# A gated cross-attention and expert layer: first norm and key stores in another order, four waits of products moved, key weights over two queues

## The chip, the cores and the metric

The kernel runs on one core of a Trainium2 chip. The metric is the device time of one execution in microseconds (us), the median of several runs. PE is the matrix engine, DVE the vector engine, ACT the scalar engine, POOL GpSimd, and SP the sync engine, which only issues transfers. PEld is PE's loading of stationary operands. ACTq, SPq and POOLq are the same engines' queues of DMA issues.

## What is computed

x has 8 sequences of 512 rows of 512 numbers, the context 8 sequences of 120 rows of 512. Cut to what matters:

```python
xn = layernorm(x)
Q = heads(xn @ Wq.T + bq); K = heads(ctx @ Wk.T + bk); V = heads(ctx @ Wv.T + bv)   # 16 heads of 32
a  = softmax(Q @ K.T / sqrt(32)) @ V
e  = mean over 8 experts of (a @ We[i].T + be[i])
x  = x + tanh(g_xattn) * (e @ Wo.T + bo)
hs = layernorm(x).reshape(4096, 512)
probs = softmax(hs @ w_gate); best = argmax(probs)       # 8 experts
keep the first 100 rows of each expert, in order of rows; gate = probs[best]
out = x + tanh(g_ffn) * (gate * (hs @ w_expert + b_expert) for the kept rows, else 0)
```

## The kernel before

Every product in full precision is made of three products of float16 parts (high by high, high by low, low by high), each 128 by 128 against up to 512 columns. The mean over the experts and Wo are folded into one 512 by 512 matrix ("mix"). Each engine runs its own list of steps in the order written in the kernel, and steps of different engines meet at semaphores (`wait_ge`).

**Prologue.** The list `units` (lines 369 to 656) holds 52 first and 6 late units. A unit is some transposes or products by PE into one of eight PSUM banks, and then a cast of the high part by ACT and the low part by DVE. A bank is taken again by the unit eight places later, once its casts are over. In order: the four tiles of Wk turned, the bias rows, the context tiles turned, K of sequences 0 to 3 (lines 459 to 479), Wv, K of sequences 4 to 7, Wq, V of sequence 0, Wo (`woT`, four units), `wogT` (line 522, Wo by the gate's weights), V of sequences 1, 2 and 3, the first sequence's normalised rows x tiles 0 and 1 turned (`x_unit`), `wog` (line 545, which reads `wogT`'s two parts), V of 4 (`v4`), `cb` (which reads `wog`), `bias_part`, x tiles 2 and 3, V of 5, `mix_bias`, V of 6. The late units are V of 7, the mix matrix in four parts, and `gateT`. They are woven into the first steps of sequence 0.

SP issues the loads (lines 734 to 766): the four Wk tiles of 256 KB, the context, and then the other weights, x and the eight experts' weights. POOL sums the experts' weights (`sum_we`), and after the first of these sums makes the first sequence's `rstd` and `x0_shift`. ACT issues the loads of three bias vectors (lines 1235 and 1236), goes through its casts of the units (lines 1274 to 1282), and has three other pieces of work between them:

- `store_k(half)` (lines 1238 to 1246): 12 DMA issues that write K's parts to DRAM, from where SP loads them as a stack. `first_units_over` (line 664) waits for all 24 of them. PE calls it ahead of the second Q product of sequence 0, and SP, POOL and DVE call it too, at the end of the prologue.
- `first_rows()` (lines 1259 to 1268): two small scalings of `tanh_g`, and the four activations that normalise the first sequence's rows into `xn`, once `x0_shift` is there.
- `be_part_high()`, a cast.

```python
if units[i]["done"] == made["wogT"]:
    store_k(1)
    first_rows()
prepare(0, i)
```

**A sequence.** For each sequence b the attention is done in four groups g of four heads. `scores` (line 879) makes the scores of a group in four banks, in two halves. The first half waits for ACT's first half of exponentials of the group before (`s_ex2`), the second for their second half (`s_ex`). `exp` on ACT turns them into `probs`. `weight_sums` (line 899) sums the weights into `den_b`, and `value_sums` (line 915) makes the weighted values in `num_b`. In the first call, (0, 0), `weight_sums` waits with `prologue_over` (line 670) for all late units. The products of sequence b+1's Q and the routing (`route_x`, line 948; `gate_mix`, line 930, in sequence 0, which waits for ACT's `part_x`) are woven between. Sequence by sequence DVE chooses each row's expert, `places` (line 1083) counts the rows per expert on PE after DVE's `choose` (`base_cnt`), DVE reads the counts (`read_places`: `place_all`), makes `place_hot`, and PE adds to a table of rows (`table_rows`, for sequence 6 split in `table_token` and `table_values`, lines 1109 to 1118).

**The tail.** In sequence 7's list (line 1215) PE also does the expert's product for the kept rows of the first seven sequences (`row_product`, 0 to 7, 12 products each, rows gathered by POOL), and then `last_product` for the last sequence's rows in five parts. Each needs a result of DVE (`row_out`) that frees its bank. DVE's and ACT's own lists for that stretch stand at lines 1866 and 1417. POOL scatters the rows and SP stores the last sequence.

PE's steps in sequence 7 begin with

```python
(scores, 0, 1), (weight_sums, 0, 0), (table_token, -1, 0), (value_sums, 0, 0), (scores, 0, 2),
```

and the end of the row products is

```python
(row_product, 0, 6), (places, 0, 0), (row_product, 0, 7), (last_product, 0, 0), ...
```

Of the kernel before, what the change touches and what calls it, by code (L numbers as in the profile page):

```python
# [49 lines left out]
P = 128  # L50
# [35 lines left out]
def build(nc, x, ctx, g_xattn, g_ffn, Wq, bq, Wk, bk, Wv, bv, We, be, Wo, bo, w_gate, w_expert, b_expert, out):  # L86
# [8 lines left out]
    with ExitStack() as st:  # L95
# [631 lines left out]
        def _(e):  # L727
# [6 lines left out]
            def load_tiles(n, w):  # L734
                for i in range(NK):
                    load(slots[slot_of[n]][:, i, :], w[i * P:(i + 1) * P, :], s_wt[n][i])

            load_tiles("wkT", Wk)
# [99 lines left out]
        def _(e):  # L838
# [60 lines left out]
            def weight_sums(b, g):  # L899
                e.wait_ge(s_ex, 4 * b + g + 1)  # L900
                if g == 0:
                    if b == 0:
                        prologue_over(e)
                    e.wait_ge(s_lraw, b)
                    e.wait_ge(s_sh, b + 1)
                for h in range(2):
                    sel = den_sel[:, (h * NK + g) * DK:(h * NK + g + 1) * DK]
                    for j in range(HJ):
                        row = slice(j * DK, (j + 1) * DK)
                        ins = mm(den_b[row, 0:SH], sel, probs[:, g % 2, j, h * SH:(h + 1) * SH],  # L910
                                 start=(g == 0 and h == 0), stop=(g == NK - 1 and h == 1))
                if g == NK - 1:
                    ins.then_inc(s_den, 1)

            def value_sums(b, g):
                if (b, g) == (B - 1, 3):
                    e.wait_ge(s_ex, 4 * B)
                elif g:
                    e.wait_ge(s_num, 4 * b + g)
# [28 lines left out]
            def route_x(b, _):  # L948
# [6 lines left out]
                if b == 0:  # L955
                    e.wait_ge(s_route, 3)
                elif b == 1:
                    e.wait_ge(s_qhi, 4)
                    e.wait_ge(s_qlo, 4)
# [245 lines left out]
            def last_product(_, i):  # L1205
# [10 lines left out]
                (scores, 0, 1), (weight_sums, 0, 0), (table_token, -1, 0), (value_sums, 0, 0), (scores, 0, 2),  # L1216
# [7 lines left out]
                (places, 0, 0), (row_product, 0, 7),  # L1224
# [6 lines left out]
        def _(e):  # L1231
            def act(out_, in_, func=ACT.Copy, **kw):
                return e.activation(out_, in_, func, **kw)  # L1233

            for i, b_ in enumerate((bq, bk, bo)):
                e.dma_start(bias_rows[i * NK:(i + 1) * NK, :], b_.rearrange("(t p) -> t p", p=P)).then_inc(s_bqk, 16)
# [37 lines left out]
            for i in range(N_FIRST):  # L1274
                if units[i]["done"] == made[("wvT", 2)]:
                    be_part_high()
                if units[i]["done"] == made["wogT"]:
                    store_k(1)
                    first_rows()
                prepare(0, i)  # L1280
# [781 lines left out]
```

## Time and profile before

| | |
|---|---|
| median of 3 runs | 415.07 us (415.05 to 415.48) |
| the profiled execution: its own time | 413.09 us |
| its span | 411.4 us |
| PE busy | 400.2 us, 97% of the span |
| DVE busy | 336.1 us, 82% |
| ACT busy | 228.3 us, 55% |
| POOL busy | 166.8 us, 41% |
| chain that ended last | PE 84%, DVE 6%, ACT 3%, issue 3%, DMA 1% |

Times in the rows below are from the start of the span. A timeline row gives the start in us, the length in us, the engine, the line, the operation, what it writes from what, the shape and the count, and, in square brackets, how long the engine was idle before it and what was done last of what it waited for. A row of several instructions gives the length from the first one's start to the last one's end. Idle time that ends in "issue" was ended by nothing that the profile shows. Matrix products overlap: the next one starts before the one before has ended. The granted clock is PE's share of full speed.

### The profile page before, as it was taken

To read this page: it belongs to the slowest core of one execution; us is meant where nothing else is said; L and a number is where in the kernel's file an instruction comes from. 1 tells how busy PE (TensorE), PEld (TensorE's weight loads), DVE (VectorE), ACT (ScalarE), POOL (GpSimd) and SP (SyncE) were. 2 spreads that over 40 slices of the span, in tenths; PEclk is the share of its full clock that TensorE was granted. 3 is DMA by queue.
4 is the path that set the end of the run, shared out by engine and by line. 5 is a ranking of instruction groups with operands and counts; after the bars stand their busy time and mean duration, and the time that the engine had idled before them with its cause. 6 is when DMAs were issued, how large, how long until landed. Compare 5 with 4: busy or idle time off the path is not lost.

```text
span 411.4 us, 8771 instructions
## 1 busy us (share of the span) xinstructions
PE 400.2 (97%) x3126; PEld 190.5 (46%) x3126; DVE 336.1 (82%) x683; ACT 228.3 (55%) x320; POOL 166.8 (41%) x154
## 2 busy tenths in 40 slices
PE   8999989999999999999999999999999999999987
PEld 4556554444444444444444444444444445354434
DVE  7449267886897989988998999899896688779994
ACT  5434422668465854947585485748457474774200
POOL 2028999115090347309033530803361072550460
DMA  8999981366048507824870692386059026232584
GB/s 278 325 387 398 385 320 37 81 124 169 2 102 175 199 1 160 220 95 88 148 237 3 144 228 104 71 170 235 1 131 239 4 55 174 73 114 47 107 169 148
DMA packets 65517, 63.19 MB, mean 154 GB/s; under 512 B 41765, under 2 KB 45233, under 8 KB 65475
## 3 DMA queue, kind: packets, MB, share of 16 engines
q1 hardware_dynamic: 60363, 56.19, 49.8%
q0 software_dynamic: 1632, 3.49, 3.1%
q10 hardware_dynamic: 3480, 2.96, 2.2%
q8 instruction: 26, 0.43, 0.5%
q14 instruction: 16, 0.13, 0.1%
HBM read 29.59 MB, written 12.98 MB: 103 GB/s over the span
## 4 chain that ended last, share of the span: by engine, by line
PE 84%; DVE 6%; ACT 3%; issue 3%; ACTq 1%; DMA 1%; SPq 0%; DVEq 0%
PE ps L840 71%; PE ps L456 7%; PE ps L588 3%; PE ps L405 2%; ACTq L1244 1%; DMA raw<-in_L_xattn_Wk_dram 1%; DVE xb L1565 1%; DVE rows L1820 1%; ACT xn L1233 1%; DVE bn_raw L1571 1%; ACT xb L1233 1%; DVE xn_lo L1808 1%; ACT woT_hi L397 0%; ACT mixT_hi L397 0%; DVE q_stack L1838 0%
## 5 line engine op out<-in xcount | busy, mean ns | idle before, releaser
L1233 ACT ACTIVATE probs<-ps 120x1024 f32<-120x1024 f32 x64 | 62.0, 1023 | 21.0 <-PE ps L840 20.9
L1599 DVE TENSOR_REDUCE neg_max<-ps 128x16 bf16<-128x1920 f32 x32 | 68.6, 2143 | 3.7 <-PE ps L840 3.7
L1985 POOL TENSOR_TENSOR attn_lo<-attn,attn_hi 128x512 f16<-128x512 f32 x28 | 31.8, 1158 | 92.0 <-ACT attn_hi L1233 92.0
L840 PE MATMUL ps<-xnT_hi,wqT_hi 128*128 128x512 f16 x128 | 48.6, 380 | 0.0
L840 PE MATMUL ps<-mixT_hi,attn_hi 128*128 128x512 f16 x128 | 48.6, 380 | 0.0
L840 PE MATMUL ps<-mixT_lo,attn_hi 128*128 128x512 f16 x128 | 48.5, 379 | 0.0
L840 PE MATMUL ps<-xnT_lo,wqT_hi 128*128 128x512 f16 x128 | 48.5, 379 | 0.0
L1993 POOL TENSOR_TENSOR xb<-xb,mix_bias 128x512 f32<-128x512 f32 x32 | 39.6, 1272 | 17.5 <-DVE cb_col L1542 17.5
L1233 ACT ACTIVATE q_hi<-ps,bias_cols 128x512 f16<-128x512 f32 x32 | 22.0, 688 | 31.5 <-PE ps L840 31.5
L840 PE MATMUL ps<-q_stack,k_stack 97*120 97x512 f16 x128 | 34.9, 390 | 0.1
L840 PE MATMUL ps<-probs,den_sel 120*32 120x256 f32 x512 | 34.1, 384 | 0.8 <-issue 0.8
L840 PE MATMUL ps<-probs,v_all 120*32 120x512 f32 x256 | 33.5, 595 | 0.0
L840 PE MATMUL ps<-mixT_hi,attn_lo 128*128 128x512 f16 x128 | 33.0, 380 | 0.0
L840 PE MATMUL ps<-xnT_hi,wqT_lo 128*128 128x512 f16 x128 | 32.8, 379 | 0.0
L1233 ACT ACTIVATE attn<-ps 128x512 f32<-128x512 f32 x32 | 19.0, 594 | 21.3 <-PE ps L840 21.3
L1233 ACT ACTIVATE q_stack<-q_hi 32x2048 f16<-32x2048 f16 x16 | 30.5, 1907 | 0.5
L1593 DVE SCALAR_TENSOR_TENSOR q_lo<-ps,bias_cols,q_hi 128x512 f16<-128x512 f32 x32 | 23.9, 746 | 5.2 <-ACT q_hi L1233 5.0
L1559 DVE TENSOR_TENSOR attn<-ps,attn 128x512 f32<-128x512 f32 x32 | 20.6, 685 | 7.8 <-PE ps L840 7.5
L1233 ACT ACTIVATE attn_hi<-attn 128x512 f16<-128x512 f32 x32 | 19.7, 627 | 12.6 <-DVE attn L1559 12.6
L1565 DVE SCALAR_TENSOR_TENSOR xb<-ps,xb 128x512 f32<-128x512 f32 x32 | 21.9, 683 | 2.8 <-PE ps L840 2.4
L840 PEld LDWEIGHTS ps<-q_stack,k_stack 97*120 97x120 f16 x128 | 14.4, 132 | 20.3 <-issue 11.1
L1924 POOL TENSOR_SCALAR veps<-mv 128x4 f32<-128x4 f32 x8 | 1.8, 228 | 51.0 <-DVE mv L1474 50.9
(277 smaller groups left out, 805.6 us busy)
## 6 DMA issues: line engine op xcount, KB each, us to landing
xb<-in_x_dram SPq DMA_DIRECT2D x8, 1024.0 KB, 6.6
q_stack<-q_hi SPq DMA_DIRECT2D x48, 128.0 KB, 2.4
out_dram<-xb SPq DMA_DIRECT2D x6, 1024.0 KB, 6.5
raw<-in_L_xattn_We_dram SPq DMA_DIRECT2D x5, 1024.0 KB, 11.2
q_stack<-q_lo SPq DMA_DIRECT2D x32, 128.0 KB, 2.4
xb<-in_L_xattn_We_dram SPq DMA_DIRECT2D x3, 1024.0 KB, 9.8
k_stack<-k_scratch SPq DMA_DIRECT2D x8, 360.0 KB, 4.3
k_scratch<-k_hi ACTq DMA_DIRECT2D x16, 120.0 KB, 6.7
```

What stands on the lines that cost most here:

```text
L405: ins = e.transpose(b[0:rows, i * cols:(i + 1) * cols], src_of(i), ident[0:cols, 0:cols])
L456: ins = e.matmul(out_, a(pa, k), b(pb_, k), start=(i == 0), stop=(i == len(steps) - 1))
L588: ins = e.matmul(b[:, :], left(i, o), right[j][:, o, :], start=(n == 0), stop=(n == len(steps) - 1))
L840: return e.matmul(out_, a, b, start=start, stop=stop, **kw)
L1233: return e.activation(out_, in_, func, **kw)
L1244: e.dma_start(k_scratch[bs, part * DK:(part + 1) * DK, j, :].rearrange("b d s -> d b s"), src[j * DK:(j + 1) * DK, bs, :, :].rearrange("d ...
L1559: e.tensor_tensor(attn[:, g, :], (den_b, num_b)[g % 2], attn[:, g, :], ALU.mult).then_inc(s_at, 1)
L1565: e.scalar_tensor_tensor(out=row, in0=pair_b[t % 2], scalar=1.0 / (ATTN_SCALE * MIX_SCALE), in1=row, op0=ALU.mult, op1=ALU.add).then_inc(s ...
L1593: e.scalar_tensor_tensor(out=q_lo[:, g, :], in0=pair_b[g % 2], scalar=bias_cols[:, g:g + 1], in1=q_hi[:, g, :], op0=ALU.add, op1=ALU.subtr ...
L1599: e.tensor_reduce(neg_max[:, :, :, g], quad[:, :, 0:NT * SK].rearrange("p j (t s) -> p t j s", t=NT), AX.X, ALU.max, negate=True).then_inc ...
L1985: e.tensor_tensor(attn_lo[:, g, :], attn[:, g, :], attn_hi[:, g, :], ALU.subtract).then_inc(s_alo, 1)
L1993: ins = e.tensor_tensor(row, row, mix_bias[:, :], ALU.add)
```

## The change

It has these parts:

- A. Wk's tiles 1 and 3 are issued by ACT, ahead of its three bias loads. SP issues tiles 0 and 2.
- B. On ACT `first_rows()` is moved to before the cast of `woT`'s first tile, and `store_k(1)` to after `wogT`'s cast.
- C. `weight_sums(0, 0)` on PE waits for the last of the four mix units and no longer for all late units. The wait for all of them is made ahead of `route_x(1)`, the first use of the bank of `gateT`.
- D. In sequence 7 `value_sums(7, 0)` is done before `table_token`, with a wait for DVE's reading of the counts of sequence 6, which are in the same bank.
- E. `places(7)` comes after `row_product` 7 and no longer before it.

```diff
-            def load_tiles(n, w):
-                for i in range(NK):
+            def load_tiles(n, w, tiles=range(NK)):
+                for i in tiles:
                     load(slots[slot_of[n]][:, i, :], w[i * P:(i + 1) * P, :], s_wt[n][i])
 
-            load_tiles("wkT", Wk)
+            load_tiles("wkT", Wk, (0, 2))
...
                 if g == 0:
                     if b == 0:
-                        prologue_over(e)
+                        for s_, n in made[("mix", NK - 1)]:
+                            e.wait_ge(s_, n)
...
             def value_sums(b, g):
                 if (b, g) == (B - 1, 3):
                     e.wait_ge(s_ex, 4 * B)
+                elif (b, g) == (B - 1, 0):
+                    e.wait_ge(s_plr, B - 1)
                 elif g:
                     e.wait_ge(s_num, 4 * b + g)
...
                 if b == 0:
                     e.wait_ge(s_route, 3)
                 elif b == 1:
+                    prologue_over(e)
                     e.wait_ge(s_qhi, 4)
                     e.wait_ge(s_qlo, 4)
...
             run([B - 1], [
-                (scores, 0, 1), (weight_sums, 0, 0), (table_token, -1, 0), (value_sums, 0, 0), (scores, 0, 2),
+                (scores, 0, 1), (weight_sums, 0, 0), (value_sums, 0, 0), (table_token, -1, 0), (scores, 0, 2),
...
-                (places, 0, 0), (row_product, 0, 7),
+                (row_product, 0, 7), (places, 0, 0),
...
+            for i in (1, 3):
+                e.dma_start(slots[slot_of["wkT"]][:, i, :], Wk[i * P:(i + 1) * P, :]).then_inc(s_wt["wkT"][i], 16)
             for i, b_ in enumerate((bq, bk, bo)):
...
+                if units[i]["done"] == made[("woT", 0)]:
+                    first_rows()
+                prepare(0, i)
                 if units[i]["done"] == made["wogT"]:
                     store_k(1)
-                    first_rows()
-                prepare(0, i)
```

## Rows read from the trace of the kernel before

**Rows 1.** Stretches: PE, PEld, DVE, ACT, POOL busy us; clock; DMA share; GB/s.

```profile
1.90:5.00 3.10, 3.10 (x15) 1.53 (x13) 2.65 (x15) 1.87 (x3) 1.52 (x10) 1.00 0.94 274
95.00:351.00 256.00, 255.88 (x2210) 115.03 (x2202) 224.11 (x451) 161.72 (x215) 93.72 (x90) 1.00 0.49 124
```

**Rows 2.** List of waits, PE alone: us in total, times, longest us.

```profile
PE ps L840 <- DVE base_cnt L1650: 1.7, 1, 1.7
...
PE ps L840 <- DVE place_hot L1721: 1.0, 1, 1.0
```

**Rows 3.** Timeline, 39 to 54 us: start us, us, engine, line, operation.

```profile
39.16 0.24 POOL L1972 TENSOR_SCALAR x_shift<-x_shift 128x4 f32<-128x4 f32 x1
...
41.50 0.31 ACTq L1244 DMA_DIRECT2D k_scratch<-k_hi  x1
...
46.19 1.79 ACTq L1244 DMA_DIRECT2D k_scratch<-k_lo  x4
...
48.36 2.93 ACT L1233 ACTIVATE xn<-xb,x_shift,rstd 128x512 f32<-128x512 f32 x4
...
51.87 0.69 DVE L398 SCALAR_TENSOR_TENSOR sum_lo<-ps,sum_hi 128x512 f16<-128x512 f32 x1 [8.41 <-ACT sum_hi L397]
...
52.81 0.17 PE L534 MATMUL ps<-gate_sum,sum_hi 128*128 128x8 f16 x1 [1.63 <-ACT xnT_hi L397]
...
53.58 0.40 PE L456 MATMUL ps<-mixT_hi,ctxT_hi 128*120 128x512 f16 x1 [0.42 <-DVE v_all L492]
```

**Rows 4.** Tile k_lo's DMAs up to 60 us; timeline of POOL and PE.

```profile
DMA to landing us min/median/max: 7.0/9.5/12.4
...
63.00 4.51 POOL L1960 TENSOR_TENSOR w_sum<-w_sum,xb 128x2048 f32<-128x2048 f32 x1
...
66.83 0.38 PE L840 MATMUL ps<-xnT_hi,wqT_hi 128*128 128x512 f16 x1
```

**Rows 5.** Timeline, DVE, PE and ACT, 92 to 102 us.

```profile
92.29 0.75 DVE L599 SCALAR_TENSOR_TENSOR mixT_lo<-ps,mix_scale,mixT_hi 128x512 f16<-128x512 f32 x1 [1.32 <-ACT mixT_hi L598]
93.32 0.75 DVE L610 SCALAR_TENSOR_TENSOR part_lo<-ps,gate_scale,part_hi 128x512 f16<-128x512 f32 x1 [0.28 <-ACT part_hi L609]
...
94.28 1.07 PE L840 MATMUL ps<-probs,den_sel 120*32 120x256 f32 x16 [0.81 <-issue]
...
100.32 0.59 ACT L1233 ACTIVATE part_x<-ps 128x512 f32<-128x512 f32 x1
...
101.64 0.17 PE L840 MATMUL ps<-gate_sum,part_hi 128*128 128x8 f16 x1
```

**Rows 6.** Timeline, ACT and PE's weight loads, 354 to 357 us.

```profile
354.75 1.92 ACT L1233 ACTIVATE probs<-ps 120x1024 f32<-120x1024 f32 x2
...
356.72 0.18 PEld L840 LDWEIGHTS ps<-q_stack,k_stack 97*120 97x120 f16 x2 [0.39 <-ACT probs L1233]
```

**Rows 7.** Timeline, PE and DVE, 390 to 398 us; DVE's waits from 372 us.

```profile
392.31 1.03 PE L840 MATMUL ps<-wqT_hi,q_stack 128*128 128x512 f16 x4
...
395.14 0.38 PE L840 MATMUL ps<-wqT_hi,q_stack 128*128 128x512 f16 x1
...
397.72 0.38 PE L840 MATMUL ps<-wqT_hi,q_hi 128*128 128x512 f16 x1
...
390.49 0.74 DVE L1826 SCALAR_TENSOR_TENSOR rows<-ps,coef,rows 100x512 f32<-100x512 f32 x1
...
394.89 0.75 DVE L1826 SCALAR_TENSOR_TENSOR rows<-ps,coef,rows 100x512 f32<-100x512 f32 x1
...
DVE xb L1863 <- PE ps L840: 2.7, 4, 1.2
```

**Rows 8.** Timeline, SP's issues and PE, the first 12 us.

```profile
0.79 1.89 SPq L729 DMA_DIRECT2D raw<-in_L_xattn_Wk_dram  x4
...
5.87 0.63 PE L405 MATMUL ps<-ident,raw 128*128 128x128 f32 x4 [0.80 <-DMA raw<-in_L_xattn_Wk_dram]
...
11.33 0.37 PE L456 MATMUL ps<-ctxT_hi,wkT_hi 128*128 128x480 f16 x1
```

## The prediction

> **What bounds the kernel now.** I read the busy times by stretch first: from 95 to 351 us PE works 255.88 of 256 us, and the next engine, DVE, 224.11 [rows 1]. So the end is set by PE's work and by the gaps in it, and moves only if a gap closes. Then the list of what PE waited for [rows 2]: eight entries, the longest 1.7 us. They lie in the prologue, at the turn to sequence 7 and in the tail, and each part of the change lies at one of them. The third view, the timelines around each gap, says what ended it and what comes next. They are needed because a gap that closes is worth only the time until the next late thing. The granted clock of 1.00, 2.4 GHz [rows 1], leaves nothing to the clock.
>
> **The change, part by part.** The sums are made against the profiled execution (span 411.4 us, its own time 413.09 us); the median of the runs shown is 415.07, 1.98 us above it, and I carry savings over unchanged.
>
> *Part B, first rows' norm ahead of the key stores.* PE's 1.6 us gap before the `wog` unit is a wait for `wogT`'s casts, not for the xn casts that the list names: `wogT` ends on DVE at 51.87+0.69 = 52.56 us, and PE starts at 52.81, after 1.63 us idle [rows 3]. Those casts sat on ACT behind 12 store issues (from 41.50 to 47.98 us) and four norm activations (2.93 us) [rows 3]. After the change ACT first does the norm. Its two tiny scalings fit while ACT still waits for `woT`'s transposes; the last input, `x0_shift`, is ready at 39.16+0.24 = 39.40 us [rows 3]. So the norm runs 39.4 to 42.35, the four `woT` casts (some 0.5 us each) to 44.4, `wogT`'s cast to 45.0, and DVE's low parts end by about 46.1. PE asks at 52.81-1.63, about 51.2, five us later. `woT`'s casts, 2.2 us later than before, free banks that PE takes again only for the x tiles, near 50; the cover is `wogT`'s product and three value products. The gap closes: 1.63 us. Behind it PE shows 0.42 us more before `v4`, at 53.58 [rows 3]. By the code `v4` has fifteen waits, all satisfied by then; the other value products have as many and none shows such a gap, so I read it as the sequencer's time, seen only because PE stood. It goes with the stall. I take 2.05, low bound 1.63.
> What is late next: the 12 store issues (6.5 us) now start at 45.0 and end near 51.4, and x tiles 0 and 1 are cast only then, until 52.5. DVE ends `wog`'s column near 53.4; PE needs it after `v4`, at 51.3+2.6 = 53.9. Slack half a microsecond. The stores end 3.4 us later; those of `k_lo` took 9.5 us to land in the median and 12.4 at most [rows 4], so 63.8 at worst, and PE comes to the wait on all stores at 66.83-2.05 = 64.8 [rows 4]. SP's loads of K, POOL's memset of `k_stack` and DVE stand behind the same wait, with one microsecond of slack or more. POOL's expert sum ends at 63.00+4.51 = 67.5 [rows 4] and doesn't move; ACT reads it only after the casts of the first two Q products and the routing, the second of which PE begins at 64.8 now, so about 69; 1.5 us in time.
>
> *Part C, the prologue's wait.* The sums of weights of sequence 0 wait for all late units, the last of which DVE ends at 93.32+0.75 = 94.07; PE starts at 94.28 after 0.81 us of idleness. Now they wait for the last mix unit alone, which DVE ends at 92.29+0.75 = 93.04, before PE's scores end at 94.28-0.81 = 93.47 [rows 5]. The 0.81 closes, but other engines don't move here: ACT's cast of the routing part stands at 100.32+0.59 = 100.91 behind norm work that doesn't depend on PE, and `gate_mix`, at 101.64 before, would now ask at 100.8 [rows 5]. That takes back about 0.16. I take 0.65; ends 0 (ACT's and DVE's pace takes all) and 0.85. The full wait, now ahead of the next routing product, two score steps later, was met at 94.07 and costs nothing.
>
> *Part D, sequence 7's first value products ahead of the token table.* PE stood 1.0 us for DVE's `place_hot` [rows 2]; now the products fill that. But the scores of g=3 need the exponentials of g=2: ACT starts those at 354.75, right behind a small exponential that waits for DVE's `l_sub`, and ends at 354.75+1.92 = 356.67. PE's second half of those scores starts at 356.72 [rows 6]: it waits for ACT already. None of these inputs is moved by D, so PE arrives a microsecond earlier and stands there. Worth 0; ends 0 and 1.0. The added wait is for `place_all`, which DVE makes before `place_hot`; behind it stand only the value products and the table, which has to wait for `place_hot` in any case.
>
> *Part E, row product 7 ahead of `places`.* PE stood 1.7 us for DVE's counts. Row product 6's last matmuls start at 392.31, four at 0.216 us, so row product 7 can start at 393.17 and not at 395.14; its input rows and its bank's reader are done (DVE's fourth row, 390.49+0.74) [rows 7]. It takes 397.72-395.14 = 2.58 us, `places` 0.1, and the last products start at 395.85 and not at 397.72: 1.87 us. They need row 4 from DVE, 394.89+0.75 = 395.64 [rows 7], just in time. DVE reads `places` only after three more row outputs, as before. Is DVE the bound then? In the tail it waited 2.7 us in all for PE [rows 7], more than 1.87, so PE still leads, by 0.8 us. I take 1.85, low bound 0.9 (row outputs late), high bound 1.95.
>
> *Part A, Wk tiles on two queues.* PE waited for tile 2, whose transposes start at 5.87 [rows 8]. Tile 2's issue comes one place earlier (issues are 0.47 us apart: 1.89 us for four [rows 8]), tile 3's two places earlier; 0.45 us is the gain if issue limits. But from 1.9 to 5.0 us the DMA engines are 94% busy at 274 GB/s [rows 1]: bytes limit as much as issues. The Trainium skill, "DMA: Bandwidth & Descriptors", section "Issuing engines are not separate DMA queues", says that DMAs issued on several engines interleave on the same 16 DMA engines and save only issue time. By that rule tile 0 would land with tile 1 and tile 2 with tile 3. Interleaved, tile 2 lands when tile 3 does now; PE's transposes of tile 3 take their turn 0.63 us after those of tile 2 began [rows 8], so the loss is at most about 0.6 us. From 5.87 to 11.33 PE runs without a real gap, so either shift passes on whole. Between -0.45 and +0.6 I take 0, since both ends are about as near. The bias rows, now two issues later on ACT, are used only behind tile 3's transposes; ACT's table load, two issues later too, has the wait of ACT's first cast for PE as its cover.
>
> **Sum:** 2.05+0.65+0+1.85+0 = 4.55 us; 413.09-4.55 = 408.5 for the profiled execution, 415.07-4.55 = **410.5 us** for the median. After 95 us PE has no gap to take the savings up until 351, and DVE, ACT and SP follow PE's steps there.
>
> **Rivals.**
> 1. *The tiles interleave*. For: the DMA shares. Against: SP's issues are still spared. PE's transposes of tiles 2 and 3 come 0.6 later: 410.5+0.6 = 411.1. Chance 0.22. It is the rule of the Trainium skill's page on DMA that stands behind this case.
> 2. *C is swallowed*: ACT's and DVE's work on the norm of sequence 2 isn't moved and PE meets it. For: DVE's norm waits for POOL there. Against: PE meets that chain in one place only by my reading. 410.5+0.65 = 411.2. Chance 0.12.
> 3. *B only moves the wait*: the stores' issue takes longer or x casts come later than PE's 53.9, and the `wog` column becomes what is late. Against: half a microsecond of slack. All of 2.05 lost: 410.5+2.05 = 412.6. Chance 0.11.
> 4. *D is worth its microsecond*, if ACT's small exponential comes earlier than I think: 410.5-1.0 = 409.5. Chance 0.08.
> 5. *Slower*: the stores. ACT issues them 3.4 us later into DMA engines that still carry the expert weights, and PE, SP, POOL and DVE all wait for the last one before sequence 0. The price is nothing until it lands after 64.8, and each microsecond later costs one; it turns the balance at 64.8+4.55 = 69.4 us, 18 us after its issue, where the slowest now takes 12.4. For 416.5 it would take 20 us. Chance 0.03.
> 6. *The change doesn't do what it says*, no gap closes: 415.1. Chance 0.02.
>
> **How the numbers follow.** The forecast, A even and the other gaps closed as summed, has the rest, 0.42. The range 409.3 to 412.2 holds it with rivals 1, 2 and 4, 0.84 together, and leaves out rival 3. A difference under 0.2% (0.8 us) can't be told from none. Faster by more: forecast and rivals 1 to 4, 0.95; within 0.2%: 0.02; slower: 0.03.
>
> **What would show it.** Right: no PE wait before `wog` and before `v4`, twelve stores issued from 45 us on; the sums of weights of sequence 0 right behind the scores, a wait of 0.1 to 0.2 at `gate_mix`; about 0.7 us of idle PE before the g=3 scores of sequence 7 in place of 1.0 before the table; no PE wait near 388 (393 before), last products without a gap. Wrong: a PE wait for `wog`'s DVE column, any new PE wait between 60 and 350 us, a wait for rows in the last products, or PE's first K product more than 0.3 us later than its 11.33 now.

## The result and the profile after

The changed kernel takes **408.98 us** in the median (407.06 to 409.04, 5 runs); the kernel before, with the two runs that were added to the three shown ahead, 415.05 us (412.36 to 415.48, 5 runs). The ratio is 0.9852, 95% interval 0.9813 to 0.9891: 6.1 us less, 1.5%. The prediction was 410.5 with a range of 409.3 to 412.2: the direction was right, the size too small, and the result lies below the range.

The profiled execution of the changed kernel took 407.45 us with a span of 405.9 (before 413.09 and 411.4), 5.64 us less. First its page and PE's list of waits (us in total, times, longest):

```profile
span 405.9 us, 8772 instructions
...
PE 398.9 (98%) x3126; PEld 190.4 (47%) x3126; DVE 336.0 (83%) x683; ACT 227.7 (56%) x320; POOL 166.9 (41%) x154
```

```profile
PE ps L855 <- POOL ones_bf L1903: 1.1, 1, 1.1
PE ps L405 <- DMA bias_rows<-in_L_xattn_bo_dram: 1.0, 1, 1.0
PE ps L840 <- ACT probs L1237: 0.8, 2, 0.5
PE ps L405 <- DMA raw<-in_L_xattn_Wk_dram: 0.5, 1, 0.5
PE ps L840 <- issue: 0.2, 1, 0.2
PE ps L456 <- DVE mixT_lo L398: 0.2, 1, 0.2
```

The waits for `base_cnt` (1.7 us) and `place_hot` (1.0) [rows 2] are gone, and so is the one ahead of `wog`. New are a wait of 1.0 us for the bias rows and two for ACT's exponentials. The timeline at the old `wog` gap, to be held against [rows 3]:

```profile
39.70 2.94 ACT L1237 ACTIVATE xn<-xb,x_shift,rstd 128x512 f32<-128x512 f32 x4 [1.81 <-POOL x_shift L1979]
42.27 0.31 ACTq L1250 DMA_DIRECT2D k_scratch<-k_hi  x1
...
45.61 0.68 DVE L398 SCALAR_TENSOR_TENSOR sum_lo<-ps,sum_hi 128x512 f16<-128x512 f32 x1
46.76 2.61 ACTq L1250 DMA_DIRECT2D k_scratch<-k_lo  x4
...
49.88 1.04 PE L405 MATMUL ps<-ident,xn 128*128 128x128 f32 x8
50.76 0.17 PE L534 MATMUL ps<-gate_sum,sum_hi 128*128 128x8 f16 x1
...
50.96 0.41 PE L456 MATMUL ps<-mixT_hi,ctxT_hi 128*120 128x512 f16 x1
```

`wogT` is ready at 46.29 and not at 52.56, PE asks at 50.76, and `v4` follows `wog` after 0.20 us. Then the other places, for [rows 5], [rows 6] and [rows 7], and DVE's waits in the tail:

```profile
90.79 0.64 PE L840 MATMUL ps<-probs,den_sel 120*32 120x256 f32 x8
...
98.35 0.18 PE L840 MATMUL ps<-gate_sum,part_hi 128*128 128x8 f16 x1
...
351.41 1.92 ACT L1237 ACTIVATE probs<-ps 120x1024 f32<-120x1024 f32 x2
...
352.47 0.64 PE L840 MATMUL ps<-q_stack,k_stack 97*120 97x512 f16 x2 [0.50 <-ACT probs L1237]
353.38 0.64 PE L840 MATMUL ps<-q_stack,k_stack 97*120 97x512 f16 x2 [0.27 <-ACT probs L1237]
...
391.55 1.03 PE L840 MATMUL ps<-wqT_hi,q_stack 128*128 128x512 f16 x4
392.41 0.18 PE L840 MATMUL ps<-choice,tri 128*128 128x32 bf16 x1
...
392.46 0.38 PE L840 MATMUL ps<-wqT_hi,q_hi 128*128 128x512 f16 x1
...
DVE xb L1870 <- PE ps L840: 1.0, 2, 0.8
```

Idle times in the list overlap with the modelled end of the last product, so I set the two traces against each other by **starts of the same PE instruction**. These are the distances, in us, and what changed:

| stretch, PE start to PE start | before | after | change |
|---|---|---|---|
| start of the span to the first K product | 11.33 | 11.07 | -0.26 (A) |
| first K product to the x tiles | 38.82 | 38.81 | -0.01 |
| x tiles to `v4` | 3.43 | 1.08 | -2.35 (B) |
| `v4` to the first sums of weights | 40.70 | 39.83 | -0.87 (C) |
| sums of weights to `gate_mix` | 7.36 | 7.56 | +0.20 (C, given back) |
| `gate_mix` to sequence 7's logits | 241.70 | 241.65 | -0.05 |
| logits to the table's products | 13.86 | 13.86 | 0 (D) |
| table's products to the last products | 40.52 | 38.60 | -1.92 (E) |
| last products to DVE's last end | 11.07 | 11.07 | 0 |
| from there to the end of the span, and outside it | 4.30 | 3.92 | -0.38 (A, see the end of "Why the prediction was wrong") |

The sum, 5.64, is that of the profiled executions. The median fell by 0.43 more, which this table can't show; that is the second half of the study.

### The profile page after: what moved, and what is told of

It is laid out like the page before. It is cut to its first block, busy times and chain, and to the rows that moved or that the text cites. A ratio compares the mean times of both kernels' runs of the same rounds, so it can differ in the third digit from the quotient of the medians.

```text
span 405.9 us, 8772 instructions
## 1 busy us (share of the span) xinstructions
PE 398.9 (98%) x3126; PEld 190.4 (47%) x3126; DVE 336.0 (83%) x683; ACT 227.7 (56%) x320; POOL 166.9 (41%) x154
## 4 chain that ended last, share of the span: by engine, by line
PE 93%; DVE 2%; ACT 1%; DMA 1%; issue 1%; ACTq 1%; POOL 0%; DVEq 0%
PE ps L840 77%; PE ps L456 9%; PE ps L588 3%; PE ps L405 2%; DMA bias_rows<-in_L_xattn_bo_dram 1%; ACT probs L1237 1%; ACT mixT_hi L397 0%; PE ps L1164 0%; DVE xb L1572 0%; DVE mixT_lo L398 0%; POOL known L1933 0%; PE ps L606 0%; PE ps L525 0%; PE ps L855 0%; ACTq L1240 0%
```

## The experiments, part by part

Every kernel here is the kernel before or after with the lines shown. They ran in five sets, with the kernel before beside them in each; its median was 415.02, 415.81, 414.43, 414.77 and 414.83 us. A table of results stands at the end of the section after this one.

**A alone** (Wk's tiles 1 and 3 on ACT's queue, no other part).

> Part A alone on the kernel before. Theory 1 (read from the changed kernel's trace): tile 0 lands later, PE's first transposes start near 4.3 and not 3.6, the bias rows land near 7.8 and PE waits 1.0 us for them, and the first K product starts at 11.1 for 11.33: a gain of 0.3 us in the profile, of 0.2 to 0.5 in the median. Theory 2 (the two queues also calm the start of the load stream, which is why the medians moved 6.1 us and the profiles 5.5): a gain of 0.8 to 1.5 us in the median. Theory 3 (interleaving as forecast at worst): a loss of 0.5 us.

Measured: 413.46 us median (411.93 to 416.46, 10 runs), ratio 0.9975 (0.9946 to 1.0003), profiled 412.81. The start:

```profile
4.38 0.64 PE L405 MATMUL ps<-ident,raw 128*128 128x128 f32 x4 [0.59 <-DMA raw<-in_L_xattn_Wk_dram]
...
7.28 0.20 PE L405 MATMUL ps<-ident,bias_rows 12*128 12x12 f32 x1 [0.51 <-DMA bias_rows<-in_L_xattn_bo_dram]
...
10.49 0.36 PE L456 MATMUL ps<-ctxT_hi,wkT_hi 128*128 128x480 f16 x1
...
52.94 0.17 PE L534 MATMUL ps<-gate_sum,sum_hi 128*128 128x8 f16 x1 [2.17 <-ACT xnT_hi L397]
```

Tile 0 is 0.76 us later than before (3.62), no tile keeps PE waiting after that, and the K products start 0.84 us earlier. At `wog` nothing of it is left: 52.94, before 52.81. There ACT's stores and norm set the time, and PE only waits 0.5 us longer. "Either shift passes on whole" held only with B beside it. The median is 1.6 us lower all the same, though the profile is lower by 0.3; what moves it is told with the clock below (seven of these ten runs kept it, one in three of the kernel before do), and whether A has a part in that stayed open. The 0.84 us itself can't be put down to A from this trace; see the starts of the other traces below.

**B alone.**

> Part B alone. Theory 1: PE's gaps there are longer from start to start than the list of waits says (1.78 and 0.57 us, not 1.63 and 0.42); v4 starts 2.35 us earlier than in the kernel before, at 51.2, and the time falls by 2.3 us. Theory 2 (my forecast, the listed idle times): 2.05 us. Theory 3: B needs A's or others' help, and gives under 1.7 alone.

Measured: 410.93 (410.45 to 411.38, 6 runs), ratio 0.991 (0.9879 to 0.994), profiled 410.95. From the x tiles to `v4` 1.08 us, as in the full change: B is worth 2.35 in the profile, of it 1.78 at `wog` (2.66 to 0.88) and 0.57 at `v4` (0.77 to 0.20). But its median is 4.1 us under the kernel before, nearly twice that, and the runs lie within 0.9 us where the kernel before spreads over 4. That was the first sign that a trace of one execution of the kernel before doesn't show all that its gap costs.

**The gap ahead of v4.** The kernel before, `v4` without its waits, all of which units ahead have made already:

```diff
-                for s_, n in u["needs"]:
+                for s_, n in [] if u["done"] == made[("v", 4)] else u["needs"]:
                     e.wait_ge(s_, n)
```

> The kernel before, without the fifteen waits of unit v4 (all on counts that PE has waited for before, in the units ahead). In the kernel before v4 starts 0.77 us after wog, with B 0.20 after. Theory of the prediction (the 0.57 is the sequencer's time for these waits, seen only because PE stood): the distance from wog to v4 falls to about 0.2 to 0.3 and the time by 0.5, to about 412.6 in the profile. Rival (the time is the fetch of instructions or something else behind a stall): it stays at 0.7 to 0.8. It also is one more sample of the stores' issue in the kernel before: 6.5 to 7.5 us and the wog unit at 52.8 to 53, or, by theory 1 of e10_stores_behind, up to 4 us later in an execution whose time is over 414.

Measured: one run, 412.48 us.

```profile
52.38 0.17 PE L534 MATMUL ps<-gate_sum,sum_hi 128*128 128x8 f16 x1 [1.37 <-ACT xnT_hi L397]
...
52.59 0.41 PE L456 MATMUL ps<-mixT_hi,ctxT_hi 128*120 128x512 f16 x1
```

`v4` stands 0.21 behind `wog` and not 0.77. So the fifteen waits, all met, took PE's sequencer 0.56 us, which shows where PE has run dry and the sequencer isn't ahead of it.

**The two halves of B.** The stores behind `wogT`'s casts, the norm at its old place:

```diff
                 if units[i]["done"] == made["wogT"]:
-                    store_k(1)
                     first_rows()
                 prepare(0, i)
+                if units[i]["done"] == made["wogT"]:
+                    store_k(1)
```

> The kernel before, with the key stores of the second half issued behind wogT's casts and not ahead of them, and ahead of them still the norm of the first rows, at its old place. Open is why the medians of the kernels with B lie some 4 us under the kernel before, while the profiled executions differ by 2.2. Theory 1 (the issue of the stores is what varies): the 12 DMA issues on ACT take 6.5 to 7.5 us and longer in many executions, and the kernel before pays every excess at the wog unit. Here they are off that path, though the norm (2.9 us) stays on it: norm and casts end near 45.5, PE asks at 51.2, so the distance from the x tiles to v4 is 1.1 us as in B alone, the profiled time near 411, the median 411 and the runs within 1 us of one another. Theory 2 (the spread comes from the start or from elsewhere, and B's excess in the median is chance): the profile is the same, but the runs spread over 4 us like those of the kernel before, with a median near 413.

The norm ahead of `woT`, the stores at their old place:

```diff
+                if units[i]["done"] == made[("woT", 0)]:
+                    first_rows()
                 if units[i]["done"] == made["wogT"]:
                     store_k(1)
-                    first_rows()
                 prepare(0, i)
```

> The other half of B: the norm of the first rows ahead of woT's casts, the 12 stores still ahead of wogT's casts. Without the norm between, wogT's high part comes 2.9 us sooner than 51.2, at about 48.3, and its low part at 49.7; PE asks at 51.2. With stores of 6.5 to 7.5 us the gap closes in the profile as in B (x tiles to v4 1.1 us). Theory 1 (the issue of the stores varies by up to 4 us between executions): 1.5 us of slack are not enough for the slow ones, so the runs spread more than in e10_stores_behind and the median lies 0.5 to 2 us above it, 411.5 to 413. Theory 2 (the norm was the costly part and the issues are steady): the same as in e10_stores_behind, median near 411, spread under 1 us.

Measured: 410.59 (410.17 to 411.5, 6 runs; ratio 0.9883, 0.9856 to 0.991) and 410.72 (410.18 to 411.87, 6 runs; 0.988, 0.9853 to 0.9906). Either half alone closes the gap (x tiles to `v4` 1.08 and 1.33 us) and makes the runs narrow. Stores and norm together are too long for the cover, each one alone is not. The theory that the stores' issue swings by up to 4 us between executions wanted the second kernel slower and wider; it isn't, so that theory falls: their issue took 6.2 to 7.7 us in all nine traces with twelve stores and norm in the old order. In the second kernel `v4` stands 0.46 us behind `wog`, though the list shows no wait before `wog`; that some of the fifteen waits' time shows there too is likely, not tested.

**All parts but D.**

> The changed kernel without part D. Theory 1: D is worth nothing; PE waits 1.0 to 1.4 us for place_hot before the token table of sequence 7, and the scores of g=3 end where they do with D; the time is within 0.2 us of the changed kernel's. Theory 2: D hides the 0.37 us that PE loses just before sequence 7's first scores, so without it the time is 0.3 to 0.5 us longer. Theory 3: D is worth the whole wait, 1.0 us longer without it.

Measured: 408.72 (407.34 to 409.15, 4 runs), ratio 0.9857 (0.9812 to 0.9902).

**D alone.**

> Part D alone. The prediction gave it nothing: PE no longer waits for place_hot (1.0 us), but the g=3 scores of sequence 7 wait for ACT's exponentials of g=2, so from the logits to the table 13.9 us as before, profile 413.1 and a median as of the kernel before. Rival: 1.0 us faster, if ACT's exponentials start sooner when PE isn't held up. One more sample of the wog gap.

Measured: 415.21 (413.01 to 416.06, 10 runs), ratio 1.0008 (0.998 to 1.0036). Logits to table 13.97 us without D in the one and 13.96 with it in the other, 13.86 in the traces before and after: no gain from D shows.

**E alone.**

> Part E alone. From the token table's values to the last products 40.52 us before; with E 38.6: 1.92 us, and nothing else moves, since it is the last part of the program: profile 411.2, median 1.9 under that of the kernel before (413.2 for 415.1). Rival (DVE leads in the tail once the gap is gone): 0.9 to 1.5. One more sample of the wog gap.

Measured: 412.3 (410.82 to 414.02, 10 runs), ratio 0.9947 (0.9921 to 0.9974), 2.1 us less; in the trace 38.61 us from the table's products to the last ones, 1.91 less.

**C alone**, measured twice.

> Part C alone. From v4 to the first weight sums 40.70 us before; with C 39.8, and 0.2 comes back at gate_mix: 0.67 in all, so a profile near 412.4 and a median 0.7 under that of the kernel before in the same call (414.4 for 415.1). Rival (with the gap at wog still there the late units stand otherwise and the whole 0.87 or nothing stays). One more sample of the wog gap.

> Part C alone once more. Its first four runs took 414.06, 415.23, 818.91 and 1427.73 us, the last two at a granted clock of 1.00, which no theory here explains. If that was a disturbance of the chip, all runs now lie between 411.8 and 416, with a median 0.7 under the kernel before in this call. If it is C's doing without B (a wait met late by a DMA), some run again takes far longer. The time from v4 to the first weight sums is 39.8 us in an execution without a fall of the clock, against 40.70.

Measured: the first time 414.06, 415.23, 818.91 and 1427.73 us. The second time 414.14 (412.2 to 415.83, 10 runs), ratio 0.9981 (0.995 to 1.0012), 0.7 us under the kernel before beside it, as the term says, but inside the interval; it is the trace and not the median that shows C's gain. The two long runs did not come back in ten; what made them was not found, and nothing rests on them. `v4` to the sums of weights took 41.35 and 41.50 us in C's two traces, where 39.8 was expected. That is the next thing.

## The experiments on the spread

The profiles of C alone (spans 412.3 and 412.6) and of D alone (414.3) have what the one before lacks: the granted clock falls behind the `wog` gap. D alone, PE's timeline, and stretches of it (PE busy us, clock, DMA share, GB/s):

```profile
54.36 0.17 PE L534 MATMUL ps<-gate_sum,sum_hi 128*128 128x8 f16 x1 [2.17 <-ACT xnT_hi L397]
...
56.00 0.38 PE L456 MATMUL ps<-mixT_lo,ctxT_hi 128*120 128x512 f16 x1
...
56.54 0.63 PE L456 MATMUL ps<-mixT_hi,ctxT_hi 128*120 128x512 f16 x1
56.97 0.63 PE L456 MATMUL ps<-mixT_lo,ctxT_hi 128*120 128x512 f16 x1
```

```profile
54.00:58.00 4.00, 3.22 (x18) 0.79 1.06 406
58.00:62.00 4.00, 3.93 (x42) 0.78 0.76 287
62.00:66.00 4.00, 4.00 (x20) 1.00 0.01 4
```

The same in the trace before:

```profile
54.00:58.00 4.00, 3.89 (x42) 1.00 1.06 406
58.00:62.00 4.00, 4.00 (x24) 1.00 0.42 160
```

PE stood for 2.17 us, went on for 1.9 us at full clock, and then products of 512 columns came 0.43 us apart instead of 0.216: 1.2 GHz in place of 2.4. Microsecond by microsecond the clock is 0.66 from 56 to 57 us, 0.50 to 59, 0.64 to 60 and then 1.00. The value products and mix units behind it are 1.42 us longer here (42.12 us to the sums of weights, 40.70 before). The Trainium skill, "TensorE: Matmul & The Clock Gate", "Part 1: The HAM clock gate", says that the lower clock is the default and that activity releases it. These rows agree: the clock falls behind the one long gap in the middle of the kernel and comes back while PE is busy.

Each run has its mean granted clock, so the runs of the kernel before can be sorted, 107 of them from the five sets and from the kernel before again:

| mean clock | runs | median us | from, to |
|---|---|---|---|
| 0.999 to 1.000 | 35 | 413.39 | 412.42 to 414.43 |
| 0.995, 0.996 | 58 | 415.22 | 413.99 to 417.39 |
| 0.991, 0.992 | 13 | 416.84 | 416.30 to 418.03 |

(One run more took 465 us at a clock of 0.849 and is left out.) A mean clock lower by 0.004 in a time of 413 us is about one such fall: 0.004 x 413 = 1.7 us lost, and the medians are 1.8 apart. The profiled execution of the kernel before, 413.09, belongs to the third without a fall; the three runs shown, 415.05 to 415.48, all took longer than any of the 35 without one. Of the 55 runs of kernels in which the gap is closed, by B or a half of it, 54 have a clock of 0.999 or 1.000.

**The kernel before again**, for a second trace and more runs.

> The kernel before, unchanged, for a second profiled execution of it and a second distribution of its times. Open is why its runs lie at 412 to 418 with a median near 415, while its profiled execution took 413.09 and those of kernels with the same order at the wog unit 412.8 (A alone) and 412.5 (v4 without its waits). Theory 1 (typical executions pay a longer stretch of store issues ahead of the norm): a profile of 414 or more shows the x tiles to v4 longer than 3.4 us by what its time is over 413. Theory 3 (profiled executions are faster than the timed ones at this place): the profile is again near 413 and the median near 415. Rival (the start of the run, the loads of Wk and the context): a slow profile shows its excess ahead of the first K product at 11.3 us.

Measured: 415.39 (412.58 to 417.53, 12 runs), ratio 1.0009 (0.9978 to 1.004). The profiled one had 413.64, clock 1.000, and a `wog` gap of 2.86 where the first had 2.66; its first K product is 0.40 later, from a wait for a context tile. So it was again an execution without a fall, which shows nothing of the slower ones.

**The gap 0.3 us shorter**, the last store issue moved behind `wogT`'s casts (`store_k` takes a range of its twelve issues):

```diff
                 if units[i]["done"] == made["wogT"]:
-                    store_k(1)
+                    store_k(1, 0, 11)
                     first_rows()
                 prepare(0, i)
+                if units[i]["done"] == made["wogT"]:
+                    store_k(1, 11, 12)
```

> The kernel before, with only the last of the twelve store issues moved behind wogT's casts: the gap at wog is shorter by one issue, 0.45 to 0.7 us (1.0 to 1.6 left of 1.6 to 2.2). Theory (clock): the granted clock stays at 0.999 to 1.000 in nearly all runs and the median falls by 1.5 to 2.5 us, three times and more the time taken off the gap: 412.5 to 413.3. Rival (the spread comes from elsewhere): median 0.5 us lower, low-clock runs as often as in the kernel before.

Measured: 414.39 (412.79 to 416.77, 12 runs), ratio 0.9997 (0.9971 to 1.0023). Five runs without a fall, seven with: no fewer falls than the kernel before had (seven of 16 without in this set). In its trace x tiles to `wog` are 2.37 us and not 2.66; the eleven issues left took 6.2 us where twelve had taken 6.5. A miss: the expectation was 1.5 to 2.5 us, and cutting the gap a little bought nothing that shows.

**The gap longer**, one norm activation done twice:

```diff
                 e.wait_ge(s_x0s, 2)
+                act(xn[:, 0, :], xb[:, 0, 0, :], ACT.Identity, scale=rstd[:, 0, 0:1],
+                    bias=x0_shift[:, 0:1]).then_inc(s_tanh, 1)
+                e.wait_ge(s_tanh, 3)
```

> The kernel before, with the first norm activation done twice (with a wait between) ahead of wogT's casts: 0.8 to 1.0 us more on ACT's chain into the wog gap. Theory (clock): this gap is where the granted clock falls (idle of 2.16 and 2.17 us before wog in the two profiles that show the fall, 1.3 to 2.2 in five that don't), and the fall costs 1.5 us more. Lengthened to 2.5 to 3 us, nearly all runs show a clock of 0.996 or less, and the median rises by more than 0.9: by 1.5 to 2.5 us over the kernel before in this call. Rival (the low clock of the runs comes from another place, as e14_gap_shorter with its 0.3 us shorter gap and 7 of 12 runs low may say): the share of low-clock runs stays near 6 in 10 and the median rises by 0.9.

Measured: 416.38 (413.84 to 418.38, 12 runs), ratio 1.0035 (1.0008 to 1.0062), 1.55 us over the kernel before, where the added activation alone would give 0.8 to 1.0. One run of 12 without a fall (in the kernel before 4 of 23 in this set, 35 of 106 in all), six of 12 at 0.991 or 0.992 (4 of 23). Its trace, in which x tiles to `wog` are 3.50 us:

```profile
53.40 0.17 PE L534 MATMUL ps<-gate_sum,sum_hi 128*128 128x8 f16 x1 [2.17 <-ACT xnT_hi L397]
...
54.16 0.65 PE L456 MATMUL ps<-mixT_hi,ctxT_hi 128*120 128x512 f16 x1 [0.41 <-DVE v_all L492]
```

```profile
50.00:54.00 4.00, 1.50 (x17) 0.94 1.06 396
54.00:58.00 4.00, 3.84 (x12) 0.63 1.06 406
58.00:62.00 4.00, 3.89 (x45) 1.00 0.62 228
```

More falls with the longer gap, as the theory said, and in one run of 55 alone where it is closed: the falls hang on this gap. From the x tiles to `wog` the traces with the old order that kept the clock show 2.37, 2.41, 2.66, 2.86, 3.04 (E alone) and 3.50 us (A alone), those in which it fell 3.06 and 3.26 (C alone), 3.50 (D alone) and 3.50 (gap longer). So the fall goes with the long gaps, but the length alone doesn't decide on one. The gap also differs by a microsecond between executions with the same order of work: in its one trace the shortened gap is like that of `v4` without waits (2.41), the lengthened one like A's and D's. A cut of 0.3 us is small against that, which is the likely reason for the miss above. Where the second fall of the runs at 0.992 lies no trace shows.

**The changed kernel again, and all parts but A**, side by side.

> The changed kernel once more, for the second distribution of its times (407.06 and 407.45, and three at 408.98 to 409.04, all at clock 1.00) and a second profile. Theory: what separates the two groups by 1.6 us is the start, where with the tiles on two queues bias rows and tiles land in a varying order; a profile of 409 shows its first K product at 12.5 us where the other had 11.07, and the same steps from there on. Rival: both profiles agree at the K product and the difference lies at the scores of sequence 7 (3.77 us from the logits to them in one, 3.40 in others).

> All parts but A once more, beside the changed kernel in the same call: is A worth anything with the rest in place? Its four runs took 408.05 to 408.62, the changed kernel's five 407.06 to 409.04. If A's gain is 0 (the prediction's term), the medians agree within 0.8 and this one has the narrower spread; if the start with two queues is the better one, the changed kernel is faster by 0.5 or more in the median. Both at a clock of 1.00 in all runs, since there is no gap before wog.

> The changed kernel without part A. Theory 1 (parts add): 0.3 us longer than the changed kernel's profile, first K product at 11.33. Theory 2 (A also calms the stream): 0.8 to 1.5 us longer in the median. Theory 3: not longer.

Measured: changed kernel 408.38 (406.83 to 409.01, 6 runs; ratio 0.9839, 0.9805 to 0.9872), without A 407.97 (407.52 to 408.81, 6 runs; 0.9844, 0.9813 to 0.9876), and in an earlier set without A 408.17 (408.05 to 408.62, 4 runs; 0.9855, 0.9814 to 0.9895). A shows no gain in the median: eleven runs with it have 408.62, ten without it 408.11. With it the runs spread from 406.8 to 409.0. The new trace, span 407.5, is 1.6 us longer than the first one's, and the difference is at the start:

```profile
4.48 1.08 PE L405 MATMUL ps<-ident,raw 128*128 128x128 f32 x4 [0.69 <-DMA raw<-in_L_xattn_Wk_dram]
...
5.58 1.06 PE L405 MATMUL ps<-ident,raw 128*128 128x128 f32 x4
...
8.91 0.28 PE L405 MATMUL ps<-ident,bias_rows 12*128 12x12 f32 x1
...
12.65 0.36 PE L456 MATMUL ps<-ctxT_hi,wkT_hi 128*128 128x480 f16 x1
```

The changed kernel's first trace:

```profile
4.33 0.77 PE L405 MATMUL ps<-ident,raw 128*128 128x128 f32 x4 [0.55 <-DMA raw<-in_L_xattn_Wk_dram]
...
5.05 0.60 PE L405 MATMUL ps<-ident,raw 128*128 128x128 f32 x4
...
7.87 0.20 PE L405 MATMUL ps<-ident,bias_rows 12*128 12x12 f32 x1 [1.01 <-DMA bias_rows<-in_L_xattn_bo_dram]
...
11.07 0.36 PE L456 MATMUL ps<-ctxT_hi,wkT_hi 128*128 128x480 f16 x1
```

Four transposes take 1.06 us in the one and 0.60 in the other, and that goes on for 5 us: the first K product starts 1.58 us later, and the two executions differ by the same (409.01 and 407.45 us). The clock column says 1.00 for both in these first 10 us, so here the durations have to be read and not the column.

Two things in the other traces belong beside this. A slow first stretch isn't A's alone: in ten of the 14 traces with all tiles on SP tile 0's transposes take 1.06 to 1.09 us, though PE has not idled before them. But from 7.3 us on all 14 are at full speed, while of the four with A and six matmuls on constants two, this one and all but D, stay slow until 9.9 and 9.3 us. And the first K product of those 14 starts anywhere from 10.76 to 12.25 us, of the four with A at 10.49, 11.07, 12.22 and 12.65. So the 0.26 us that the first pair of traces gives A at the start is less than the spread.

**The bias rows first.** The changed kernel with ACT's three bias loads ahead of its two tiles:

```diff
-            for i in (1, 3):
-                e.dma_start(slots[slot_of["wkT"]][:, i, :], ...)
             for i, b_ in enumerate((bq, bk, bo)):
                 e.dma_start(bias_rows[i * NK:(i + 1) * NK, :], ...)
+            for i in (1, 3):
+                e.dma_start(slots[slot_of["wkT"]][:, i, :], ...)
```

> The changed kernel, with the three small bias loads issued on ACT ahead of Wk's tiles 1 and 3. In the changed kernel PE waits 1.0 us for the bias rows (bias unit at 7.87 us, K product at 11.07). Theory 1 (they are late because their descriptors queue behind tile 3 of Wk): now they land early and the 1.0 us goes, but tiles 1 and 3 are issued 1.0 to 1.4 us later, after the spared tile 0 has had the DMA engines for itself; tile 0's transposes start at 3.6 to 4.0, the K product at 10.3 to 11.0, profiled time 0.1 to 0.8 under the changed kernel, median near 408.0 to 408.5. Rival: tile 1 comes so late (issued at 2.3) that PE waits for it and for tile 3 and nothing is gained: K product at 11.1 to 11.6, median 409.

Measured: 411.89 (410.2 to 412.54, 6 runs), ratio 0.9905 (0.9875 to 0.9935), 3 us worse than the changed kernel.

```profile
3.58 1.07 PE L405 MATMUL ps<-ident,raw 128*128 128x128 f32 x4
...
7.66 1.09 PE L405 MATMUL ps<-ident,raw 128*128 128x128 f32 x4 [2.80 <-DMA raw<-in_L_xattn_Wk_dram]
```

Tile 0, with no tile of ACT's beside it, is there at 3.58 as in the kernel before. Tile 1, issued from 2.03 and not from 0.80 on, comes 2.8 us after PE asks for it, at 7.66, where the changed kernel had it by 5.05. SP's context tiles were issued from 1.71 on; that they took the engines first is the likely reason, and wasn't tested. The transposes stay slow past 12 us, and the first K product starts at 15.42. The rival was right, and by more than it said.

**Eight matmuls on constants ahead of tile 0**, in the changed kernel:

```diff
-WARM_FIRST, WARM_UNITS = 6, 7
+WARM_FIRST, WARM_UNITS = 8, 7
```

> The changed kernel with eight instead of six of the matmuls on constants that PE does before the first tile. In two profiles with part A (spans 407.5 and 407.2) the transposes of tile 0, behind an idle of 0.69 and 0.71 us, take 1.06 us where they take 0.60 in two others, and go on so until 9 to 10 us; the first K product starts at 12.65 and 12.22 there and at 11.07 and 10.49 in the others. Theory: PE's clock rises late when PE idles before tile 0; two more matmuls (0.43 us each) fill 3.79 to 4.65, the transposes run at full speed in all executions, and the times keep to the faster group, 407.0 to 407.6, with a first K product at 11.0 to 11.4: median 407.4 against the changed kernel's 408.4 to 409.0 and 408.0 without A. Rival (the clock at the start has nothing to do with that idle, its phase is chance): still two groups, or all 0.2 later because tile 0 waits for the matmuls, median 408.5.

Measured: **407.45** (406.99 to 407.72, 6 runs), ratio 0.9817 (0.9784 to 0.985), the fastest kernel of the study, 1.2 us under the eleven runs of the changed kernel (408.62), which ran in other sets.

```profile
4.50 0.95 PE L405 MATMUL ps<-ident,raw 128*128 128x128 f32 x4
...
5.39 0.60 PE L405 MATMUL ps<-ident,raw 128*128 128x128 f32 x4
...
10.61 0.37 PE L456 MATMUL ps<-ctxT_hi,wkT_hi 128*128 128x480 f16 x1
```

PE doesn't idle before tile 0, tile 1's transposes are at full speed, and no run falls into the group at 409, where six of the eleven are. The theory held; that the idle before tile 0 is what prolongs the slow stretch rests on these six runs and on the five traces with A.

The results together:

| kernel | median us | lowest to highest, runs | span of the profile |
|---|---|---|---|
| A alone | 413.46 | 411.93 to 416.46, 10 | 411.3 |
| B alone | 410.93 | 410.45 to 411.38, 6 | 409.2 |
| C alone, again | 414.14 | 412.20 to 415.83, 10 | 412.6 |
| D alone | 415.21 | 413.01 to 416.06, 10 | 414.3 |
| E alone | 412.30 | 410.82 to 414.02, 10 | 409.4 |
| all but D | 408.72 | 407.34 to 409.15, 4 | 407.2 |
| all but A, again | 407.97 | 407.52 to 408.81, 6 | 405.8 |
| all, again | 408.38 | 406.83 to 409.01, 6 | 407.5 |
| all, eight matmuls first | 407.45 | 406.99 to 407.72, 6 | 405.5 |

## Why the prediction was wrong in size and right in kind

Faster by more than 0.2%, at 0.95, was right, and so was the mechanism of parts B to E. The step that failed is the first of the sums: *"the median of the runs shown is 415.07, 1.98 us above it, and I carry savings over unchanged"*. The 1.98 us were no constant between a profiled and a timed run. They are a fall of PE's clock that two in three executions of the kernel before pay behind the `wog` gap and the profiled one did not. "The granted clock of 1.00 leaves nothing to the clock" was read from two stretches of that one execution [rows 1]. B closes the gap and takes the fall with it. After the change the median again lies above the profiled execution, by 408.98-407.45 = 1.53 us, but for another reason, the slow start.

The result lies 1.54 us under the forecast. Of this 0.45 is the offset, 1.98 before and 1.53 after, and 1.09 is in the profiles, 5.64 where the sum had 4.55: B's term is short by 0.30, A's by 0.64 (0.26 at the start and 0.38 at the end), E's by 0.07, the rest by 0.08. With the offset unchanged the 5.64 would have given 409.4 us, inside the range, so it is this step that took the result out of it. That it cost only 0.45 is luck: 1.98 us went with the fall and 1.53 came with the slow start, and the prediction had neither. The range's low end had no bound for this offset, nor one for B above 2.05.

- **B, 2.05 forecast, 2.35 in the trace, 4.1 in the median.** The gaps were read as idle times, 1.63 and 0.42 [rows 3]. From start to start they shrink by 1.78 and 0.57, since a product's modelled end lies some 0.16 us past the next one's earliest start. That the second gap is the sequencer's time was right (v4 without waits). Wrong in detail: the stores were to run from 45.0 to 51.4. They began at 42.27, while ACT's casts still ran until 45.04, because ACT's queue issues ahead of ACT, and ended at 49.4. Rival 3 and rival 5, which hung on late stores, had even less room than they were given: PE has no wait but 0.2 us between 60 and 350.
- **C, 0.65 forecast, 0.67 measured** (0.87 closed, 0.20 back at `gate_mix`), at the very place that was named.
- **D, 0 forecast, 0 measured**, with PE waiting for ACT's exponentials at 352.47 and 353.38, 0.77 us in all where 0.7 was forecast, in place of `place_hot`.
- **E, 1.85 forecast, 1.92 measured**, and DVE's waits for PE fell from 2.7 [rows 7] to 1.0, so PE still leads in the tail.
- **A, 0 forecast, no gain in the median**, by luck, since the zero stood between two bounds and not for these effects. Rival 1 had the mechanism: both queues' tiles share the DMA engines, as the Trainium skill, "DMA: Bandwidth & Descriptors", "Issuing engines are not separate DMA queues", says; tile 0 comes 0.7 us later and PE idles before it. Its price, 0.6 us at tiles 2 and 3, was wrong: once begun, the four tiles come without a pause. In six of eleven runs of the changed kernel the start costs some 1.6 us more, as the one trace of such a run shows. "The bias rows are used only behind tile 3's transposes" missed that, issued behind tile 3, they may come later than its transposes end, by 1.0 us in the first trace.
- **A at the end of the program, not forecast.** From DVE's last step to the end of the span the six traces with A have 2.37 to 2.45 us, the 14 without 2.51 to 2.61; and a run's time exceeds its span by 1.46 to 1.63 us in all 37 runs with A, by 1.68 to 1.86 in all without. So the 0.38 us there come with A. Why loads issued at the start should shorten the end stays open.

## What to carry to other kernels

Hold the profiled execution's time and its granted clock against those of the timed runs before making a sum: if they differ, part of what is to be predicted isn't in the trace, and runs sorted by their mean clock say what it is. A gap of PE can cost its own length and a fall of the clock behind it, so closing it whole can be worth nearly double (here 4.1 for 2.35 us), and shortening it by 0.3 us nothing. Where a load is moved so that PE's first work comes later, try filling the time with matmuls on constants (1.2 us here). A small load behind a large one can be late, by 0.5 and 1.0 us here, but moving it ahead isn't free: it cost 3 us. And one trace of each kernel doesn't give a term of 0.3 us at the start, where fourteen traces of one order lie 1.5 us apart.

## What the runs showed of the hardware that was not expected

- After an idle of 2.17 us PE went on at full clock for 1.9 us (D alone) and then at half for some 3 us; with the same idle A alone kept its clock, and with the longer gap the first product was already at half.
- At the start four transposes took 1.06 us in place of 0.60, for up to 5 us, while the clock column showed 1.00.
- With A the time of a run exceeds its span by 0.2 us less, in all 37 runs.
- Fifteen waits that are all met cost PE 0.56 us when it had run dry, 0.04 us each if all cost the same.
- A tile of 256 KB issued 1.2 us later, when the other queue had begun on the context tiles, came at least 2.6 us later (bias rows first).
